# Three result banks, four places for staged weights, shifted beats and a split copy-out in a dynamic-convolution and mixture-of-experts block on one core

## What is computed

```
x = x + involution(layernorm(x))        # 7x7, 16 groups of 8 channels
    r    = relu(batchnorm(x @ w_reduce))            # 128 -> 32
    kgen = r @ w_span + b_span                      # 49 weights for each pixel and group
    out[pixel, g, c] = sum_k kgen[pixel, g, k] * patch[pixel, k, g, c]
x = x + moe(layernorm(x))               # 8 experts, top 2 of the softmax
    y = sum_e w_e * (gelu(x @ W1[e] + b1[e]) @ W2[e] + b2[e])
```

## Time and profile before

| | us |
|---|---|
| median of 3 runs | 1218.68 |
| lowest, highest | 1218.61, 1230.3 |
| profiled execution | 1210.05 |
| its span | 1208.3 |
| TensorE busy (matmul) | 902.9 |
| VectorE, ScalarE, POOL busy | 502.4, 557.6, 488.9 |

### The profile page before, as it was taken

The page is one execution under the profiler, slowest core; times in us unless marked ns, Lnnn a source line. Parts: engine busy times, 40 slices in busy tenths (PEclk is TensorE's granted clock), DMA queues, the critical chain, the costliest instruction groups (busy, mean ns, idle before and its releaser), DMA issues. The chain is left out here.

```text
span 1208.3 us, 29680 instructions
## 1 busy us (share of the span) xinstructions
PE 902.9 (75%) x11249; PEld 807.0 (67%) x11249; DVE 502.4 (42%) x1612; ACT 557.6 (46%) x1198; POOL 488.9 (40%) x536
## 2 busy tenths in 40 slices
PE   2586479878889968998888988799798877725720
PEld 1475367768778867887778877788787766614620
DVE  6111234225444645345454463545544364504432
ACT  4343244455645555464555637455554435302410
POOL 3000010721055740757227570366406571567145
PEclk9577777789988979888789888898888996767875
DMA  6757661717255553737537375363645232223312
GB/s 145 151 122 221 130 147 44 182 51 179 60 147 140 137 145 78 191 104 171 134 70 203 83 186 120 94 170 95 145 95 146 79 81 68 73 73 86 107 49 67
DMA packets 184078, 144.04 MB, mean 119 GB/s; under 512 B 65110, under 2 KB 169558, under 8 KB 183488
## 3 DMA queue, kind: packets, MB, share of 16 engines
q1 hardware_dynamic: 168114, 115.03, 38.9%
q0 software_dynamic: 14336, 25.72, 8.1%
q10 hardware_dynamic: 1486, 1.38, 0.5%
HBM read 89.70 MB, written 52.36 MB: 118 GB/s over the span
## 5 line engine op out<-in xcount | busy, mean ns | idle before, releaser
L562 POOL DMA_INDIRECT xrows<-tn,pos x224 | 215.7, 963 | 304.7 <-DVE pos L929 175.5
L699 ACT ACTIVATE hT<-hy,staged 128x128 f32<-128x128 f32 x490 | 153.0, 365 | 302.7 <-PE hy L1214 302.4
L653 ACT ACTIVATE kb<-kg 112x896 f32<-112x896 f32 x224 | 205.7, 918 | 175.2 <-PE kg L1110 174.7
L1110 PE MATMUL kg<-rT,wk 98*112 98x112 f32 x1792 | 265.3, 313 | 28.0 <-ACT kb L653 25.3
L576 POOL DMA_INDIRECT got<-yrows,pos x224 | 213.7, 954 | 161.5 <-issue 76.5
L1110 PEld LDWEIGHTS kg<-rT,wk 98*112 98x112 f32 x1792 | 230.3, 204 | 51.4 <-ACT kb L653 38.2
L1214 PE MATMUL hy<-xT,staged 128*128 128x128 f32 x980 | 188.1, 323 | 65.1 <-DVE yo L956 43.5
L1144 PE MATMUL e<-kb,win 112*32 112x64 f32 x6272 | 200.9, 291 | 48.0 <-ACT kb L653 24.9
L1144 PEld LDWEIGHTS e<-kb,win 112*32 112x32 f32 x6272 | 170.1, 131 | 67.5 <-ACT kb L653 30.3
L1214 PEld LDWEIGHTS hy<-xT,staged 128*128 128x128 f32 x980 | 152.9, 223 | 86.1 <-DVE yo L956 49.2
L947 DVE COPY staged<-table 128x642 f32 x245 | 124.6, 509 | 189.3 <-DVE yo L956 176.1
(11 more groups left out here) (113 smaller groups left out, 654.5 us busy)
## 6 DMA issues: line engine op xcount, KB each, us to landing
win<-xpad SPq DMA_DIRECT2D x56, 784.0 KB
xin<-xrows SPq DMA_DIRECT2D x56, 256.0 KB
yrows<-yo SPq DMA_DIRECT2D x56, 256.0 KB
t_row<-in_x_dram SPq DMA_DIRECT2D x64, 112.0 KB
xpad<-xs SPq DMA_DIRECT2D x240, 28.0 KB
out_dram<-t_row SPq DMA_DIRECT2D x56, 112.0 KB
xs<-in_x_dram SPq DMA_DIRECT2D x48, 112.0 KB
xrows<-tn SPq DMA_DIRECT2D x4, 896.0 KB, 7.4
```

Source lines behind the costliest of these rows:

```text
L562: pool.indirect_dma_start(xrows[n % 2], bass.IndirectOffsetOnAxis(ap=pos[n % 2][:, i:i + 1], axis=0), tn[:, c * C:(c + 1) * C], None) \
L653: act.activation(kb[:, lo:lo + 8 * PATCHES].rearrange("p (h k) -> p h k", h=2), kg[0:WIN, :].rearrange("p (h k) -> p h k", h=2)[:, :, 0:4 ...
L699: ins = act.activation(hT_at(n, i)[:, f * 128:(f + 1) * 128], h_at(i)[:, f * 128:(f + 1) * 128], ACT.Gelu, bias=staged_at(n, i)[:, 2 * HID ...
L1110: mm = pe.matmul(kg_bank[j % 2][0:WIN, i * PATCHES:(i + 1) * PATCHES], wk[:, at:at + WIN], r[:, :, :, b4 + i], start=True, stop=True, skip ...
```

## The change

- **Banks.** `hy` gets a third bank and `e` keeps one. Visit i waits for the result of three visits before (`bank_read`), and `apply` t+1 for `take_conv` t. The last band writes its second products to `hy` as the others do; `in_tail` goes.
- **Weights.** Four `staged` places, staged three tiles ahead. Their room comes from `tnT`, which now shares the buffers of `xnT` and `r_lin`, with waits for that.
- **Visits.** `VISITS` has beat 1 in place of 7, and a visit at beat 0 of a quarter stands ahead of the `apply` there, on TensorE and VectorE.
- **Copy-out.** Of the last four kernel pairs of a quarter, ScalarE copies only bank 0 (448 columns) and VectorE bank 1, as the first thing of beats 9, 11, 13 and 15. TensorE waits for both, with a new semaphore `kb_dve`.
- **Bursts.** `moments` is split into its statistics and its small operations, a beat apart. `top_two`, `top_second` and `places` are cut into seven parts at beats 4 to 11; `pos` comes at beat 10 instead of 8. `SCATTER` and `GATHER` move and `mix` follows a beat later.
- **Order.** `put_xn`, `load_x`, `rstd1`, `apply1` and `take_tnT` move by some beats.

The diff, cut to its core:

```diff
-    VISITS = (0, 2, 4, 6, 7, 8, 10, 12, 14)
+    VISITS = (0, 1, 2, 4, 6, 8, 10, 12, 14)
     PAIRS = (NT + 1) // 2
-    SCATTER = (9, 30)
-    GATHER = (39, 57)
+    SCATTER = (11, 32)
+    GATHER = (39, 58)
...
-        tnT = [sb(f"tnT{i}", [128, 4 * T]) for i in range(2)]
+        tnT = [xnT, r_lin]
...
-        staged = [sb(f"staged{i}", [128, ROW]) for i in range(3)]
+        staged = [sb(f"staged{i}", [128, ROW]) for i in range(4)]
...
-        e_bank = [bank("e0"), bank("e1")]
+        e_bank = bank("e")
         misc = bank("misc")
         back = bank("back")
-        hy_bank = [bank("hy0"), bank("hy1")]
+        hy_bank = [bank("hy0"), bank("hy1"), bank("hy2")]
...
         def h_at(i):
-            return hy_bank[i % 2]
+            return hy_bank[i % 3]
 
         def turned_at(i):
 
-            return hy_bank[i % 2][:, HID:2 * HID]
-
-        def y_at(n, i):
-            return e_bank[i % 2][:, 0:C] if in_tail(n) else hy_bank[i % 2][:, HID:HID + C]
+            return hy_bank[i % 3][:, HID:2 * HID]
+
+        def y_at(i):
+            return hy_bank[i % 3][:, HID:HID + C]
...
-            return staged[(NT * n + i) % 3]
+            return staged[(NT * n + i) % 4]
 
         def bank_read(n, i):
 
-            return NT * n + max(i - 1, 0)
+            return NT * n + (max(i - 2, 0) if i else -1)
...
-                    if o == 40 and 2 * n + 4 < UNITS:
+                    if o == 43 and 2 * n + 4 < UNITS:
                         put_xn(2 * n + 4)
-                    if o == 41 and 2 * n + 5 < UNITS:
+                    if o == 42 and 2 * n + 5 < UNITS:
                         load_x(2 * n + 5)
...
-                    if o == 32 and 2 * n + 4 < UNITS:
+                    if o == 33 and 2 * n + 4 < UNITS:
                         rstd1(2 * n + 4)
-                    if o == 54 and 2 * n + 5 < UNITS:
-                        rstd1(2 * n + 5)
                     if o == 55:
                         rstd2(2 * n)
                     if o == 59:
                         rstd2(2 * n + 1)
+                    if o == 61 and 2 * n + 5 < UNITS:
+                        rstd1(2 * n + 5)
...
+                if k >= 8:
+                    act.wait_ge(gate_done, 4 * (k // 4 - 1))
...
+                if p >= 4:
+                    act.activation(kb[:, lo:lo + 4 * PATCHES], kg_bank[0][0:WIN, 0:4 * PATCHES], ACT.Copy).then_inc(kb_act, 1)
+                    return
...
-                if k >= 2:
+                if g == 0:
+                    done = min(4 * n + 8, 2 * UNITS)
+                    act.wait_ge(feat_done, done)
+                    act.wait_ge(feat_ready, done)
+                if g >= 2:
...
-                    if o in (33, 35, 37, 39) and 2 * n + 4 < UNITS:
-                        apply1(2 * n + 4, o - 33, o - 31)
+                    if o in (35, 37, 39, 41) and 2 * n + 4 < UNITS:
+                        apply1(2 * n + 4, o - 35, o - 33)
+                    if o in (59, 61):
+                        take_tnT(n, (o - 59) // 2)
                     if o in (57, 58):
                         apply2(n, o - 57)
                     if o in (61, 62):
                         apply2(n, o - 59)
-                    if o in (59, 61):
-                        take_tnT(n, (o - 59) // 2)
...
-                                        e_bank[t % 2][:, 0:4 * T].rearrange("p (g k) -> p g k", g=4),
+                                        e_bank[:, 0:4 * T].rearrange("p (g k) -> p g k", g=4),
...
+            def take_kernels(Q, p):
+
+                g = 4 * Q + p // 2
+                dve.wait_ge(kg_done, 16 * Q + 2 * p + 2)
+                if g >= GSLOTS:
+                    dve.wait_ge(main_done, 4 * ((g - GSLOTS) // 4 + 1))
+                lo = ((g % GSLOTS) * POS + 8 * (p % 2) + 4) * PATCHES
+                dve.tensor_copy(kb[:, lo:lo + 4 * PATCHES], kg_bank[1][0:WIN, 0:4 * PATCHES]).then_inc(kb_dve, 1)
...
-                if m >= 3:
-                    dve.wait_ge(y_out, m - 2)
+                if m >= 4:
+                    dve.wait_ge(y_out, m - 3)
...
-                    if i + 2 < NT:
-                        stage(n, i + 2)
-                if i >= SLOTS - 3 and n + 1 < NC:
-                    stage(n + 1, i - SLOTS + 3)
+                    if i + 3 < NT:
+                        stage(n, i + 3)
+                if i >= SLOTS - 4 and n + 1 < NC:
+                    stage(n + 1, i - SLOTS + 4)
...
+                if live and Q + 1 < QUADS * NC and j in (9, 11, 13, 15):
+                    take_kernels(Q + 1, j // 2)
                 if beat == BEATS + START - 2:
                     dve.wait_ge(expert_loaded, 16 * 6)
-                    for i in range(3):
+                    for i in range(4):
                         stage(0, i)
+                if j == 0 and visit(beat):
+                    expert_visit(*visit(beat))
                 if live and j in (6, 10):
                     add_back(Q, (j - 6) // 4)
                 if live and j in (0, 2, 4, 6):
                     take_conv(4 * Q + j // 2)
-                if visit(beat):
+                if j and visit(beat):
...
-                    if o == 27 and 2 * n + 4 < UNITS:
-                        moments1(2 * n + 4)
-                    if o == 50 and 2 * n + 5 < UNITS:
-                        moments1(2 * n + 5)
-                    if o == 54:
-                        moments2(2 * n)
-                    if o == 58:
-                        moments2(2 * n + 1)
+                    if o in (26, 27) and 2 * n + 4 < UNITS:
+                        moments1(2 * n + 4, (o - 26,))
+                    if o in (50, 51) and 2 * n + 5 < UNITS:
+                        moments1(2 * n + 5, (o - 50,))
+                    if o in (54, 55):
+                        moments2(2 * n, (o - 54,))
+                    if o in (58, 59):
+                        moments2(2 * n + 1, (o - 58,))
...
+                        top_first(n - 1)
+                    if o == 6:
                         top_second(n - 1)
-                    if o == 6:
+                    if o == 7:
+                        second_chosen(n - 1)
                         ranks(n - 1)
-                    if o == 8:
+                    if o == 9:
                         places(n - 1)
+                    if o == 10:
+                        positions(n - 1)
+                    if o == 11:
+                        experts_of_tiles(n - 1)
                 if 0 <= n - 2 < NC:
-                    for i in rows_moved(o - 2, GATHER):
+                    for i in rows_moved(o - 3, GATHER):
                         mix(n - 2, i)
...
                     pe.wait_ge(kb_act, pair)
+                    if pair >= 5:
+                        pe.wait_ge(kb_dve, 4 * (pair // 8) + max(0, pair % 8 - 4))
...
                     pe.wait_ge(kb_act, 8 * (Q + 1))
+                    pe.wait_ge(kb_dve, 4 * (Q + 1))
                 k = window_no(n, q // 2, s)
                 if q % 2 == 0:
                     pe.wait_ge(win_loaded[k % WSLOTS], 16 * (k // WSLOTS + 1))
-                if t >= 2:
-                    pe.wait_ge(conv_ready, t - 1)
+                if t:
+                    pe.wait_ge(conv_ready, t)
...
-                if in_tail(n) and i >= 2:
-                    pe.wait_ge(gelu_done, NT * n + i - 1)
-                elif bank_read(n, i):
+                if bank_read(n, i) > 0:
                     pe.wait_ge(y_out, bank_read(n, i))
...
             def second_product(n, i):
                 m = NT * n + i
                 pe.wait_ge(gelu_done, m + 1)
-                if in_tail(n):
-                    if i < 2:
-                        pe.wait_ge(conv_ready, STEPS * NC)
-                    else:
-                        pe.wait_ge(y_out, m - 1)
-                elif i % 2 == 0 and i // 2 + 1 < PAIRS:
+                if i % 2 == 0 and i // 2 + 1 < PAIRS:
                     pe.wait_ge(xT_ready, PAIRS * n + i // 2 + 2)
                 for f in range(2):
-                    mm = pe.matmul(y_at(n, i), hT_at(n, i)[:, f * 128:(f + 1) * 128],
+                    mm = pe.matmul(y_at(i), hT_at(n, i)[:, f * 128:(f + 1) * 128],
                                    staged_at(n, i)[:, HID + f * C:HID + (f + 1) * C], start=(f == 0), stop=(f == 1),
                                    skip_group_check=True)
                 mm.then_inc(y_done, 1)
...
                 more = Q + 1 < QUADS * NC
+                if j == 0 and visit(beat):
+                    expert_visit(*visit(beat))
                 if live:
                     if j < 8 and j % 2 == 0:
                         apply_wait(4 * Q + j // 2)
                         kernels(Q + 1, j - 1)
                         kernels(Q + 1, j)
                 if beat == BEATS + START - 1:
-                    turn_pair(0, 0, 1)
-                if visit(beat):
+                    turn_pair(0, 0, SLOTS - 1)
+                if j and visit(beat):
...
-                    if o == 7:
+                    if o == 8:
```

(37 more changed lines are left out.)

10 lines of the change are left out of this document (3 added, 7 removed).

## The result

| | before | after |
|---|---|---|
| median of 16 runs, us | 1218.64 | 1227.03 |
| lowest, highest | 1210.18, 1230.3 | 1219.84, 1234.68 |
| span of the profiled execution | 1208.3 | 1226.9 |

The ratio is 1.0062, with a 95% interval of 1.004 to 1.0084. The forecast was 1163 with a range of 1132 to 1203, so it was wrong in size and in sign. Differences of a few us between single chapters are therefore not settled by one pair of profiles.

What follows compares the result with a forecast made beforehand. TensorE was taken as the bound, waiting on `put_y` and ScalarE's copy-out. Chapters 2 to 4 -36.2, chapter 5 -8.4, chapters 1 and 6 -4 each, chapter 0 -1: together -53.6, giving 1163 us, range 1132 to 1203.

Steps and rivals of the forecast that it cites:

- From beat 34 to the next chapter, 59.5: Beat 34 to the next chapter's first `take_conv`: 66.7 us before, 59.5 forecast, with quarter 3 giving 6.9 back.
- TensorE waits there some 2 us: Beats 58 to 63 of quarter 3: TensorE was to wait some 2 us for VectorE amid statistics, mixes, visits and copies.
- VectorE's copy, 0.62 us: Each of VectorE's 16 copies a chapter was to take 0.62 us, 10 us a chapter; bounds 0.35 and 0.62.
- the rival in which the two take turns: If ScalarE and VectorE took turns reading PSUM, 0.54 + 0.62 = 1.16 us exceeds the present 0.92; D would follow.
- Third bank, -45: One more visit of slack was to remove 45 of TensorE's 54.8 us waiting for `put_y`; bounds 20 and 54.8.
- `stage`, 0.75 us each: On VectorE, `stage` waits 0.75 us for its own `put_y`; counted in VectorE's occupied 31.7 us of quarter 3.
- Visit ahead of `apply`: At beat 0 of a quarter, TensorE's 22.6 us waiting for ScalarE's last copy-out were to go; bounds 18 and 22.6.
- `pos` at 26.4, `xin` 44.9 later: `pos` 26.4 us into a chapter, then 44.9 us of scatters and load; TensorE waits some 6 us for `xin`.
- Chapter 0, -1, and chapter 1, -4: Chapter 0: shorter copies, -1 us. Chapter 1: half of the visits, -6, and `pos` two beats later, +2.
- One bank for `e`, 0: The single `e` bank was to cost 0: `take_conv` hidden between applies while VectorE is less than 1.3 us late.
- C: Rival: VectorE becomes the bound, kernel pairs wait for its copy, some 137 us a chapter, 1189 us; chance 0.17.
- D: Rival: later `pos` and waits on `kb_dve` eat the bank's gain; chapters 141 to 143, 1210 to 1218 us; chance 0.11.

Runs made afterwards that it cites:

- e1: The changed kernel, but ScalarE copies both banks of every kernel pair and VectorE none: 1202.0 us, 0.987 of the kernel before.
- e3: The changed kernel, with ScalarE copying both banks and weights staged two tiles ahead instead of three: 1184.5 us, 0.971 of the kernel before.
- e5: The changed kernel, but VectorE's share of the copies begins only with the kernels of chapter 1: 1224.8 us, 1.004 of the kernel before.
- e10: e1 with a VectorE reduction of 448 columns, for which nobody waits, in place of each copy from chapter 1 on: 1207.0 us, 0.989 of the kernel before.
- e6: The kernel before with three `hy` banks, one `e` bank and `in_tail` gone, all else as before: 1215.8 us, 0.998 of the kernel before.
- e2: The changed kernel, but weights are staged two tiles ahead instead of three: 1197.2 us, 0.982 of the kernel before.
- e4: The kernel before, with VectorE copying the second bank of the last four kernel pairs of a quarter: 1257.6 us, 1.030 of the kernel before.
- e7: e3 with SP storing the last results ahead of the load of the next `xin` at beat 34: 1185.7 us, 0.973 of the kernel before.
- e8: e3 with the routing back at beats 4 to 8 (`pos` at beat 8) and scatters from beat 9: 1185.6 us, 0.972 of the kernel before.
- e9: e7 with gathers and their mixes three beats earlier: 1184.0 us, 0.971 of the kernel before.
- e11: e9 with the routing and scatters of e8 (`pos` at beat 8): 1186.1 us, 0.972 of the kernel before.
- e13: e9 with the first transposes of a band at beat 36 instead of beat 34: 1167.2 us, 0.958 of the kernel before.

## Why the prediction was wrong

The forecast of a chapter was 26.4 + 44.9 + 59.5 = 131 us: up to `pos`, from there to the first transposes, and from beat 34 to the next chapter. Chapter 4 measured 27.0 + 46.9 + 69.5 = 143.4. The step that failed is the last term, and in it the price of VectorE's copies.

- **From beat 34 to the next chapter, 59.5.** It was 761.1 - 691.6 = 69.5, 10 us more, and 68.5 to 71.5 in chapters 2 to 5, 69.7 in the mean. Quarter 3 was to give 6.9 back and gave -1.5; the rest of quarter 2 was to take 23.5 and took 26.6. The 0.5 us for the clock stood against this: 35.9 us of TensorE work in the quarter at 0.76, where the earlier trace rows has 33.6 at 0.83. The mean of the same stretch is 65.8 us in e1 and 63.8 in e3, by one trace each. So some 4 of the 10 us go with VectorE's copies and 2 more with the round trip of `stage`; the last 4 are still there in e3, and their cause stays open.
- **What the copies do.** "TensorE waits there some 2 us" was 4.1 at once, and 11.7 us for the copy in the four quarters of chapter 4. I compared sums (31.7 of 34.5 us) where what counts is how late an in-order queue is at the moment of the pair. In the whole kernel this is 23 to 25 us (e1, e5, e10) of the 64 between 1163 and 1227.
- **VectorE's copy, 0.62 us.** Right, 0.618, though taken from a row of another operation: 1.38 ns a column, against 0.78 of `stage` in SBUF (501 ns for 642). It is as long also where ScalarE copies the other bank at the same moment (755.59 above, 0.62 and 0.54). So the rival in which the two take turns has no support here. The occupied time was right too: 24.5 + 9 x 0.75 = 31.3 us in quarter 3, against 31.7.
- **Third bank, -45.** The waits went, all 54.8 us. But e6 shows that removing them, at the price of one `e` bank, was worth nothing by itself. The step counted waits at one place as time. By the waits that grew in e6 (48.5 us), they belong to a lateness that TensorE meets at several places. This step, which stands behind the quarters of 34 and 28 us, was wrong in kind.
- **`stage`, 0.75 us each.** The forecast saw that "the change leaves this round trip in place" and gave it no price beyond VectorE's sum. Shortening it gained 30 us on the change (e2) and 18 to 20 without the copies (e3).
- **Visit ahead of `apply`.** Right: 22.6 to 1.5 us.
- **`pos` at 26.4, `xin` 44.9 later.** Near: 27.0 and 46.9 in chapter 4. The wait of 6 us was 1.0 there, since TensorE was itself late; in e1, without the copies, it is 6 to 9 in chapters 2 to 5.
- **Chapter 0, -1, and chapter 1, -4.** They were +9.1 and +7.3. The first is the 35 us wait, and e4 has it with the split alone (133.6). I didn't ask what VectorE is waiting for there when a kernel pair needs it; the trace of before had a wait of 32.8 us in VectorE at that place. For chapter 1, e1 has 127.8 against 130.8, so some 3 us may be the copies; the rest isn't settled, the single profiles of e7, e8, e9 and e11, all near 1185 us, have 127.1, 124.8, 129.8 and 125.2 there.
- **One bank for `e`, 0.** Right for chapters 1 to 5 of the change, wrong by itself (14.9 us in e6, 6.4 in e1, and some 20 us at once in chapter 0 of both).
- **Behind chapter 5, -4.** The rest of the span gave 3.6 us, about as forecast.

Of the rivals, C had the mechanism, and its sign came (over 8 us a chapter of waits on VectorE's copy: 8.6 in the mean, 11.7 in chapter 4), but its 137 us a chapter and 1189 were still too low. D came nearest in the chapters (141 to 143, against 143.2 in the mean), and none of the rivals had the time. The order moves, the visits and the spread bursts have no run of their own beyond e8 and e11.

## What to carry to other kernels

Before work is moved to a second engine, look at what stands ahead of it in that engine's queue, above all waits on transfers, and not at how busy it is: 92 pieces of 0.6 us cost some 5 us as plain work and 23 when TensorE waited for them. A wait that disappears at one place need not be a gain: in e6 54.8 us went at one place, waits at four others grew by 48.5, and the time stayed. What did gain here was to ask later for the result of a chain of fixed length (17 us in e13), and to use a buffer to shorten a round trip in a queue (18 to 30 us in e2 and e3).

## What wasn't expected of the hardware

One idle stretch of 4.10 us on TensorE, in 11.6 us with only 6.4 us of work, was followed by some 19 us mostly at the lower clock level, with kernel pairs at 1.72 us instead of 1.02. In the first 15 of them TensorE was busy for 13.4 us. Scaled by 1.02 to 1.72 the same work takes 7.9 us, an estimate from these rows. So what followed cost some 5 us, more than the wait itself. The forecast had seen the effect ("the clock falls for some microseconds") and priced it at 0.5 us.
